# A graph-and-expert layer on one core: blank rows written in pieces, dispatched rows in two halves, result filled later

## The chip, the cores and the metric

The kernel runs on one core of a Trainium2 chip. The metric is the device time of one execution in microseconds; before and after are each run several times, and the median is compared. One further execution is profiled. All loops are unrolled in the program except some rarely taken ones.

## The reference

Input: 3125 nodes with 256 features, 53125 weighted edges sorted by target, weights of three sub-layers, all float32.

```python
xn = layernorm(x)
x = x + gnn(xn) + mix(xn)          # two rounds of sparse product, softmax, tanh; linear attention
h = layernorm(x)
probs = softmax(h @ gate_w + gate_b)      # 8 experts
idx, prb = argmax(probs), max(probs)
pos = (place of the token among those of its expert); kept = pos < 489
buf[e, pos] = h                           # a dispatch of rows to their expert's buffer
y = relu(buf @ w1 + b1) @ w2 + b2         # for each expert: 489 x 256 -> 1024 -> 256
x = x + nan_to_num(y[idx, pos] * prb * kept)
```

## The kernel before

Nodes stand in 25 tiles of 128 (the last has 53). `XX` holds, for each node, 514 words: the normalised row (256, `XN`), the row so far, which is the residual of the last step (256, `X1`), the gate's probability (`kp`), and the node's number (`ids`).

Stages, in the order of time. *Ranking* (until about 300 us of the span): the edges are sorted into blocks and the attention's products are formed. *Build*: the adjacency matrix is made as 157 units (four 128 x 128 blocks each, by one-hot products, TensorE line 1261), evacuated by ScalarE (line 619) to `RING`, applied at once to `XN` (line 1278, first of three sparse products), and stored to `adj_dram` by ScalarE's DMA queue as 32 chunks of five units (line 623). `RING` has two chunks for this, so the evacuation of chunk n + 2 waits for the store of chunk n. VectorE makes the one-hot tiles (`hots`, lines 886 to 895) ahead of TensorE, and between them copies finished node rows to `HB` (`hn_out`, line 906). *Strips*: the matrix is read back in chunks by SyncE's DMA queue (line 466) for two more sparse products of seven strips each (line 1411). In the second, each strip's nodes are finished, gated and dispatched. *Experts*: for each of eight, rows are loaded, flipped (line 1182), multiplied up (line 1493) and down (line 1504), and VectorE finishes four blocks of the result (`yblock`, from line 1162), which POOL scatters to `out` (line 552).

The dispatch: `xbuf_dram` has 8 x 512 rows of 514 words. Rows to which no node goes must read as zero with an impossible node number, so that their results are dropped. For this POOL writes a tile `blank`, 128 x 514 words, that lies in `hb[:, 5376:5890]`, over the attention's weights `wq_n` and `woT` (dead once the small products are done, line 992), and SyncE writes it over the whole of `xbuf_dram` in one DMA (line 394). Later `HB`'s tile 21 takes the same columns; so VectorE waits for that DMA (`s_xz`, line 994, step 40 of its loop). POOL waits for it before the first dispatch, then scatters each tile's 514-word rows (line 544). SyncE waits for all dispatches (`s_disp`), loads the normalised halves of two experts (`tokens`, line 439), then their residual halves (`kept_rows`, line 442).

Nodes over an expert's capacity of 489 get no expert result. So `out` is first filled with the residual rows (`before`, lines 446 and 448): tiles 0 to 19 when strips 0 to 4 are done, the rest after the first loads; POOL's scatters wait for the fills (`s_pre`).

The order of each engine's instructions is as written; an engine that waits holds all that is behind it. The same holds for SyncE, which issues most DMAs.

Of the kernel before, what the change touches and what calls it, by code (L numbers as in the profile page):

```python
# [9 lines left out]
I32 = mybir.dt.int32  # L10
ACT = mybir.ActivationFunctionType
AX_X = mybir.AxisListType.X
ds = bass.ds
# [10 lines left out]
ROW = 2 * 256 + 2  # L24
# [71 lines left out]
def graph_program(nc, a, out):  # L96
    ctx = ExitStack()
    with ctx:
        def sb(name, shape, dt=F32):
            return ctx.enter_context(nc.sbuf_tensor(name, shape, dt))  # L100

        def sem(name):
            return ctx.enter_context(nc.semaphore(name))

        def dram(name, shape, dt=F32):
            return nc.dram_tensor(name, shape, dt, kind="Internal").ap()
# [3 lines left out]

        xbuf_dram = dram("xbuf_dram", [NE * XS, ROW])

# [30 lines left out]
        blank = hb[:, 5376:5376 + ROW]  # L143
# [87 lines left out]
        kvc = sb("kvc", [P, 2])  # L231
        M = W[:, 3364:3876].rearrange("p (c n) -> p c n", c=2)
# [112 lines left out]
        s_disp = sem("s_disp")  # L345
        s_b2 = sem("s_b2")
# [37 lines left out]
        def _(sp):  # L384
# [9 lines left out]
            sp.dma_start(xbuf_dram.rearrange("(p c) d -> p c d", p=P), blank.unsqueeze(1).to_broadcast([P, NE * XS // P, ROW])).then_inc(s_xz, 16)  # L394
# [43 lines left out]
            def tokens(e, s):  # L438
                sp.dma_start(xbs[:, s, :, 0:D], xbuf_dram[ds(e * XS, XS), 0:D].rearrange("(c p) f -> p c f", p=P)).then_inc(s_wl[s], 16)

            def kept_rows(e, s):
                sp.dma_start(xbs[:, s, :, D:ROW], xbuf_dram[ds(e * XS, XS), D:ROW].rearrange("(c p) f -> p c f", p=P)).then_inc(s_res[s], 16)

            def before(t0, t1):
                last = min(t1, NT - 1)
                sp.dma_start(out[t0 * P:last * P, :].rearrange("(t p) d -> p t d", p=P), X1[:, t0:last, :]).then_inc(s_pre, 16)
                if t1 == NT:
                    sp.dma_start(out[last * P:N, :], X1[0:LAST, last, :]).then_inc(s_pre, 16)
# [22 lines left out]
            sp.wait_ge(s_var, NS - 1)  # L471
            before(0, 20)
# [6 lines left out]
            for s in range(2):  # L479
                kept_rows(s, s)  # L480
            sp.wait_ge(s_var, NS + 1)
            before(20, NT)
# [12 lines left out]
        def _(gp):  # L495
# [31 lines left out]
            gp.wait_ge(s_mv, 1)  # L527
            gp.memset(blank, 0.0).then_inc(s_blank, 1)
            gp.wait_ge(s_blank, 1)
            gp.memset(blank[:, 2 * D + 1:ROW].bitcast(I32), NOWHERE).then_inc(s_zero, 1)  # L530
# [8 lines left out]
            gp.wait_ge(s_xz, 16)  # L539
            for k in range(NS):  # L540
                gp.wait_ge(s_slot, k + 1)
                for j in STRIPS[k]:
                    n = P if j < NT - 1 else LAST
                    gp.indirect_dma_start(xbuf_dram[:, :], bass.IndirectOffsetOnAxis(ap=sidx[0:n, j:j + 1], axis=0),  # L544
                                          XX[0:n, j, :], None, bounds_check=NE * XS - 1, oob_is_err=False).then_inc(s_disp, 16)

            gp.wait_ge(s_pre, 16 * 3)
# [9 lines left out]
        def _(act):  # L557
# [136 lines left out]

            for k in range(NS):
                zout(0, k)
                ex(0, k)
                tanh(0, k)
# [43 lines left out]
        def _(dve):  # L742
# [3 lines left out]
            def link(ins):  # L746
                chain[0] += 1
                ins.then_inc(s_dve, 1)
                dve.wait_ge(s_dve, chain[0])
# [209 lines left out]
            for it in range(NU + 8):  # L959
# [33 lines left out]
                if it == NT + 15:  # L993
                    dve.wait_ge(s_xz, 16)
# [160 lines left out]
            def yblock(e, s):  # L1155
                for c in range(4):
                    n = min(P, CAPX - c * P)
                    y = ybs[0:n, s, c, :]
                    dve.wait_ge(s_y, 4 * e + c + 1)
                    if e >= 2 and c == 0:  # L1160
                        dve.wait_ge(s_out[s], 16 * 4 * (e // 2))
                    v.tensor_tensor(y, ps[0:n, 5 + c % 2, 0:D], b2_b[0:n, e * D:(e + 1) * D], ALU.add).then_inc(s_yv, 1)  # L1162
                    dve.wait_ge(s_yv, 4 * e + c + 1)
                    link(v.tensor_scalar(y, y, xbs[0:n, s, c, 2 * D:2 * D + 1], None, ALU.mult))
# [370 lines left out]
```

## Time and profile before

| | us |
|---|---|
| median of 3 runs | 1299.79 (1293.42 to 1300.66) |
| profiled execution | 1298.54 |
| its span | 1296.6 |
| TensorE busy | 1145.2 (88%) |
| VectorE busy | 737.5 (57%) |
| ScalarE busy | 326.1 (25%) |
| POOL busy | 109.0 (8%) |
| mean granted clock of TensorE | 0.947 of full speed |

In the profile PE is TensorE, DVE VectorE, ACT ScalarE, POOL GpSimd and SP SyncE. An engine's busy time is no measure of what it costs: only what lies on the chain of work that ended last sets the time. The granted clock is a share of 2.4 GHz. Times of rows are microseconds from the start of the span.

### The profile page before, as it was taken

The numbers are of one execution on the slowest core, as the hardware profiler recorded it, in microseconds if no ns is written. First come the engines' busy times: TensorE is split into PE (matmuls) and PEld (weight loads), VectorE is DVE, ScalarE is ACT, GpSimd is POOL, SyncE is SP. The second block draws the span as 40 slices with busy tenths as digits, with TensorE's granted clock in tenths as the row PEclk, the third lists the DMA queues.
The fourth block names the chain that finished last, engine by engine and source line by source line (L and its number), as shares of the span: only waits on it lengthen the run. The fifth ranks groups of instructions, "written<-read, shape, count | busy, mean of one in ns | idle before, by whom it ended". The sixth has DMA issues, their size and how long they took to land.

```text
span 1296.6 us, 14218 instructions
## 1 busy us (share of the span) xinstructions
PE 1145.2 (88%) x4999; PEld 725.3 (56%) x4999; DVE 737.5 (57%) x1711; ACT 326.1 (25%) x1028; POOL 109.0 (8%) x150
## 2 busy tenths in 40 slices
PE   1678988889379999999999799999999649999996
PEld 1345655666146666666668344454555526676664
DVE  5888988978067777777775011022345614455544
ACT  1445445431012121121212011111322412211220
POOL 1112112110000000000000000000112111111111
PEclk9799889899679999999999899999999759999998
DMA  6100101112941112211122898878897632333320
GB/s 161 11 4 41 42 1 41 41 41 74 252 137 82 81 82 85 119 82 82 82 93 110 300 375 295 301 278 303 224 343 258 210 124 88 119 113 108 117 99 9
DMA packets 61077, 175.38 MB, mean 135 GB/s; under 512 B 15990, under 2 KB 40285, under 8 KB 48974
## 3 DMA queue, kind: packets, MB, share of 16 engines
q1 hardware_dynamic: 46504, 120.70, 27.9%
q10 hardware_dynamic: 10598, 45.72, 9.0%
q0 software_dynamic: 3904, 8.03, 2.0%
q8 instruction: 42, 0.69, 0.2%
q14 instruction: 29, 0.24, 0.1%
HBM read 113.82 MB, written 63.01 MB: 136 GB/s over the span
## 4 chain that ended last, share of the span: by engine, by line
PE 80%; DVE 7%; ACT 5%; DMA 5%; issue 2%; SPq 0%; POOL 0%; POOLq 0%; DVEq 0%; ACTq 0%
PE ps L1411 21%; PE ps L1278 19%; PE ps L1261 11%; PE ps L1493 8%; PE ps L1504 8%; DMA xbuf_dram<-HB 3%; PE ps L1236 3%; ACT W L597 2%; PE ps L1182 2%; PE ps L1303 2%; ACT RING L609 1%; PE ps L1443 1%; PE ps L1222 1%; PE ps L1280 1%; DVE W L847 1%
## 5 line engine op out<-in xcount | busy, mean ns | idle before, releaser
L1278 PE MATMUL ps<-RING,XX 128*128 128x512 f32 x600 | 284.3, 596 | 0.2
L1411 PE MATMUL ps<-RING,RY 128*128 128x512 f32 (+1 forms) x700 | 277.0, 552 | 6.4 <-issue 6.4
L1261 PEld LDWEIGHTS ps<-RING 128*128 128x128 f32 x1250 | 163.8, 194 | 84.7 <-issue 81.9
L1261 PE MATMUL ps<-RING 128*128 128x128 f32 x1250 | 171.5, 278 | 39.8 <-DVE RING L895 30.8
L1411 PEld LDWEIGHTS ps<-RING,RY 128*128 128x128 f32 x700 | 124.9, 192 | 140.7 <-issue 140.7
L619 ACT COPY RING<-ps 128x512 f32<-128x512 f32 (+1 forms) x157 | 91.6, 584 | 368.6 <-PE ps L1261 352.5
L886 DVE TENSOR_TENSOR RING<-iota_n,RY 128x512 f32<-128x512 f32 (+1 forms) x157 | 107.8, 687 | 105.1 <-PE ps L1261 60.7
L1278 PEld LDWEIGHTS ps<-RING,XX 128*128 128x128 f32 x600 | 103.2, 192 | 73.1 <-issue 73.0
L892 DVE TENSOR_TENSOR RING<-iota_n,RY 128x512 f32<-128x512 f32 (+1 forms) x157 | 106.9, 681 | 0.0
L895 DVE TENSOR_TENSOR RING<-RING,RY 128x512 f32<-128x512 f32 x132 | 89.9, 681 | 0.0
L1162 DVE TENSOR_TENSOR W<-ps,RING 128x256 f32<-128x256 f32 (+1 forms) x32 | 13.4, 419 | 126.6 <-PE ps L1504 126.6
L544 POOL DMA_INDIRECT xbuf_dram<-XX,sidx x25 | 25.6, 1023 | 702.6 <-DVE sidx L1126 696.8
L733 ACT ACTIVATE RY<-ps,b1T 128x489 f32<-128x489 f32 x64 | 42.8, 670 | 162.3 <-PE ps L1493 162.3
L1049 DVE TENSOR_REDUCE nmx<-ps 128x4 f32<-128x512 f32 (+1 forms) x7 | 4.4, 635 | 115.5 <-PE ps L1182 115.5
L1504 PE MATMUL ps<-RING,RY 128*128 128x256 f32 (+1 forms) x256 | 56.3, 381 | 0.8 <-ACT RY L733 0.8
L1504 PE MATMUL ps<-XT,RY 128*128 128x256 f32 (+1 forms) x256 | 56.3, 381 | 0.0
L1493 PE MATMUL ps<-RING,XT 128*128 128x489 f32 x128 | 55.3, 591 | 0.7 <-ACT RING L726 0.7
L1236 PE MATMUL ps<-wkvT,XT 128*128 128x512 f32 x100 | 51.1, 636 | 3.7 <-ACT XT L588 3.7
L1493 PE MATMUL ps<-RING 128*128 128x489 f32 x128 | 53.1, 573 | 0.0
L1504 PEld LDWEIGHTS ps<-RING,RY 128*128 128x128 f32 (+1 forms) x256 | 47.1, 185 | 9.5 <-ACT RY L733 1.5
L847 DVE TENSOR_TENSOR W<-HB 128x468 bf16<-128x468 bf16 x125 | 51.9, 478 | 0.0
L1504 PEld LDWEIGHTS ps<-XT,RY 128*128 128x128 f32 (+1 forms) x256 | 47.1, 185 | 8.0
(232 smaller groups left out, 1300.0 us busy)
## 6 DMA issues: line engine op xcount, KB each, us to landing
RING<-adj_dram SPq DMA_DIRECT2D x62, 1280.0 KB, 6.0
adj_dram<-RING ACTq DMA_DIRECT2D x31, 1280.0 KB, 4.5
xbuf_dram<-HB SPq DMA_DIRECT2D x1, 8224.0 KB, 43.5
XT<-in_L_ffn_w SPq DMA_DIRECT2D x8, 1024.0 KB, 7.5
RING<-in_L_ffn_w SPq DMA_DIRECT2D x8, 1024.0 KB
RING<-xbuf_dram SPq DMA_DIRECT2D x8, 516.0 KB, 4.0
RING<-xbuf_dram SPq DMA_DIRECT2D x8, 512.0 KB, 5.3
XX<-in_x ACTq DMA_DIRECT2D x1, 3072.0 KB
```

Source lines behind the costliest of these rows:

```text
L619: nc.scalar.copy(RING[:, n % 2, u % 5 * 512:u % 5 * 512 + w], ps[:, bank_of(u), 0:w]).then_inc(s_bev, 1)
L733: nc.scalar.activation(hmT[:, f, 0:CAPX], ps[:, 2 + f % 3, 0:CAPX], ACT.Relu, bias=b1T[:, f, e:e + 1]).then_inc(s_hidv, 1)
L847: last = v.tensor_tensor(V[:, b, f * SW:(f + 1) * SW].rearrange("p (c s i) -> p c s i", s=NR, i=2), ohp[b].rearrange("p (c s i) -> p c s i ...
L886: v.tensor_tensor(h[:, 0, 0:n, :], every, grid(0), ALU.is_equal).then_inc(s_eq, 1)
L892: last = v.tensor_tensor(h[:, 1, 0:n, :], every, grid(1), ALU.is_equal)
L895: last = v.tensor_tensor(h[:, 0, 0:n, :], h[:, 0, 0:n, :], grid(2), ALU.mult)
L1236: last = nc.tensor.matmul(ps[:, PROD, :], XT[:, c, m * P:(m + 1) * P], wkvT[:, c, :], start=(c == 0), stop=(c == 1))
L1261: last = nc.tensor.matmul(o[:, i * P:(i + 1) * P], h[:, 0, i, :], h[:, 1, i, :], start=True, stop=(j != s))
L1278: last = nc.tensor.matmul(ps[:, ACC + dd, :], w, at, start=(j == 0), stop=True, skip_group_check=True)
L1411: last = nc.tensor.matmul(o, (Y if l == 0 else S0)[:, j, :], RING[:, slot_of[g % 5], i * w:(i + 1) * w], start=(j == 0), stop=(j == NT - 1 ...
L1493: last = nc.tensor.matmul(ps[:, 2 + f % 3, 0:CAPX], w1s[s][:, c, f * P:(f + 1) * P], xbT[:, s, c, 0:CAPX], start=(c == 0), stop=(c == 1))
L1504: last = nc.tensor.matmul(o, hmT[:, f, c * P:c * P + n], w2s[s][:, f, :], start=(f == 0), stop=(f == 7))
```

## The change

- `blank` moves to `W[:, 2048:2562]`, is written once `s_m` is reached (the small products are done), and VectorE's wait at step 40 is gone. ScalarE waits for all blank writes before the first sparse strip, whose results go to the same columns.
- `xbuf_dram` becomes two buffers: `xbuf_dram` with 256-word rows, and `rbuf_dram` with 258-word rows for residual, probability and number. SyncE writes the blanks in eight steps, an expert's 512 rows of both buffers at a time, after ScalarE's evacuations 44, 54, ... 114.
- POOL scatters 256-word rows for a strip's tiles, then the 258-word rows; those of strip 5 come behind the dispatches of strip 6.
- SyncE loads `tokens` for two experts after the first halves, waits for the second (`s_dres`), loads `kept_rows(0, 0)`, fills all of `out`, loads `kept_rows(1, 1)`.
- `yblock` multiplies `b2` by the probability before it waits for TensorE, and then forms product and sum in one operation on the PSUM tile.

```diff
--- before.py
+++ after.py
@@ -21,7 +21,8 @@
 NE = 8
 CAPX = 489
 XS = 512
-ROW = 2 * 256 + 2
+RES = 256 + 2
+ROW = 256 + RES
 NOWHERE = 1 << 20
 F = 1024
 NH = 8
@@ -108,7 +109,8 @@
 
         adj_dram = dram("adj_dram", [NC, P, 5 * 512])
 
-        xbuf_dram = dram("xbuf_dram", [NE * XS, ROW])
+        xbuf_dram = dram("xbuf_dram", [NE * XS, D])
+        rbuf_dram = dram("rbuf_dram", [NE * XS, RES])
 
 
         XX = sb("XX", [P, NT, ROW])
@@ -140,7 +142,6 @@
         ohp = [hb[:, 4806 + 234 * i:5040 + 234 * i].bitcast(BF16) for i in range(2)]
         wq_n = hb[:, 5376:5888].rearrange("p (r n) -> p r n", r=2)
         woT = hb[:, 5888:6400].rearrange("p (r n) -> p r n", r=2)
-        blank = hb[:, 5376:5376 + ROW]
 
         recs = RY[:, 0:5 * NG].rearrange("p (f n) -> p f n", f=5)
         S0 = RY[:, 0:NT * H].rearrange("p (t n) -> p t n", n=H)
@@ -229,6 +230,7 @@
         hrs = sb("hrs", [P, 2, KT * NH])
         hta = sb("hta", [P, KT * NH])
         kvc = sb("kvc", [P, 2])
+        blank = W[:, 2048:2048 + ROW]
         M = W[:, 3364:3876].rearrange("p (c n) -> p c n", c=2)
         nmx = sb("nmx", [P, 2, 4])
         rsum = sb("rsum", [P, 2, 4])
@@ -343,6 +345,7 @@
         s_cntr = sem("s_cntr")
         s_slot = sem("s_slot")
         s_disp = sem("s_disp")
+        s_dres = sem("s_dres")
         s_b2 = sem("s_b2")
         s_wl = [sem(f"s_wl{i}") for i in range(2)]
         s_res = [sem(f"s_res{i}") for i in range(2)]
@@ -391,7 +394,11 @@
                     for to, name in ((src_w, "src"), (dst_w, "dst"), (val_w, "edge_weight")):
                         sp.dma_start(to[:, ds(j * WC, WC)], a[name][ds(first, WIN)].rearrange("(p c) -> p c", c=WC)).then_inc(s_win[g], 16)
             sp.wait_ge(s_zero, 3)
-            sp.dma_start(xbuf_dram.rearrange("(p c) d -> p c d", p=P), blank.unsqueeze(1).to_broadcast([P, NE * XS // P, ROW])).then_inc(s_xz, 16)
+            for i in range(8):
+                sp.wait_ge(s_bev, 44 + 10 * i)
+                for to, cols in ((xbuf_dram, blank[:, 0:D]), (rbuf_dram, blank[:, D:ROW])):
+                    w = D if to is xbuf_dram else RES
+                    sp.dma_start(to[i * XS:(i + 1) * XS, :].rearrange("(p c) d -> p c d", p=P), cols.unsqueeze(1).to_broadcast([P, XS // P, w])).then_inc(s_xz, 16)
 
             sp.wait_ge(s_rounds, 1)
             with more_rounds(sp):
@@ -436,10 +443,10 @@
                 sp.dma_start(w2s[s], a["L0_ffn_w2"][ds(e, 1), :, :].rearrange("a (c p) f -> p (a c) f", p=P)).then_inc(s_wl[s], 16)
 
             def tokens(e, s):
-                sp.dma_start(xbs[:, s, :, 0:D], xbuf_dram[ds(e * XS, XS), 0:D].rearrange("(c p) f -> p c f", p=P)).then_inc(s_wl[s], 16)
+                sp.dma_start(xbs[:, s, :, 0:D], xbuf_dram[ds(e * XS, XS), :].rearrange("(c p) f -> p c f", p=P)).then_inc(s_wl[s], 16)
 
             def kept_rows(e, s):
-                sp.dma_start(xbs[:, s, :, D:ROW], xbuf_dram[ds(e * XS, XS), D:ROW].rearrange("(c p) f -> p c f", p=P)).then_inc(s_res[s], 16)
+                sp.dma_start(xbs[:, s, :, D:ROW], rbuf_dram[ds(e * XS, XS), :].rearrange("(c p) f -> p c f", p=P)).then_inc(s_res[s], 16)
 
             def before(t0, t1):
                 last = min(t1, NT - 1)
@@ -468,18 +475,16 @@
                         sp.wait_ge(s_mixp, NT)
                         weights(0, 0)
 
-            sp.wait_ge(s_var, NS - 1)
-            before(0, 20)
             sp.wait_ge(s_zc, 2 * NC)
             weights(1, 1)
             sp.dma_start(b2_b, a["L0_ffn_b2"].rearrange("e d -> (e d)").partition_broadcast(P)).then_inc(s_b2, 16)
             sp.wait_ge(s_disp, 16 * NT)
             tokens(0, 0)
             tokens(1, 1)
-            for s in range(2):
-                kept_rows(s, s)
-            sp.wait_ge(s_var, NS + 1)
-            before(20, NT)
+            sp.wait_ge(s_dres, 16 * NT)
+            kept_rows(0, 0)
+            before(0, NT)
+            kept_rows(1, 1)
             for e in range(NE - 2):
                 sp.wait_ge(s_xbt, 2 * (e + 1))
                 tokens(e + 2, e % 2)
@@ -524,10 +529,10 @@
                     gp.wait_ge(s_stats, NT)
                     gp.tensor_tensor(X1[:, it, :], X1[:, it, :], bo_b[:, :], ALU.add).then_inc(s_bo, 1)
 
-            gp.wait_ge(s_mv, 1)
+            gp.wait_ge(s_m, 1)
             gp.memset(blank, 0.0).then_inc(s_blank, 1)
             gp.wait_ge(s_blank, 1)
-            gp.memset(blank[:, 2 * D + 1:ROW].bitcast(I32), NOWHERE).then_inc(s_zero, 1)
+            gp.memset(blank[:, ROW - 1:ROW].bitcast(I32), NOWHERE).then_inc(s_zero, 1)
 
             gp.wait_ge(s_rounds, 1)
             with more_rounds(gp):
@@ -536,15 +541,19 @@
                     gp.wait_ge(s_ast[i], 16 * NC // 2)
                 gp.iota(e_int, pattern=[[1, NP]], base=0, channel_multiplier=0).then_inc(m_iota, 1)
 
-            gp.wait_ge(s_xz, 16)
+            gp.wait_ge(s_xz, 16 * 16)
             for k in range(NS):
                 gp.wait_ge(s_slot, k + 1)
                 for j in STRIPS[k]:
                     n = P if j < NT - 1 else LAST
                     gp.indirect_dma_start(xbuf_dram[:, :], bass.IndirectOffsetOnAxis(ap=sidx[0:n, j:j + 1], axis=0),
-                                          XX[0:n, j, :], None, bounds_check=NE * XS - 1, oob_is_err=False).then_inc(s_disp, 16)
-
-            gp.wait_ge(s_pre, 16 * 3)
+                                          XX[0:n, j, 0:D], None, bounds_check=NE * XS - 1, oob_is_err=False).then_inc(s_disp, 16)
+                for j in STRIPS[k] if k < NS - 2 else [] if k < NS - 1 else STRIPS[k - 1] + STRIPS[k]:
+                    n = P if j < NT - 1 else LAST
+                    gp.indirect_dma_start(rbuf_dram[:, :], bass.IndirectOffsetOnAxis(ap=sidx[0:n, j:j + 1], axis=0),
+                                          XX[0:n, j, D:ROW], None, bounds_check=NE * XS - 1, oob_is_err=False).then_inc(s_dres, 16)
+
+            gp.wait_ge(s_pre, 16 * 2)
             for e in range(NE):
                 for c in range(4):
                     n = min(P, CAPX - c * P)
@@ -692,6 +701,7 @@
                 act.wait_ge(s_tb, k + 1)
                 nc.scalar.activation(ta8[:, 0:w, :], tb8[:, 0:w, :], ACT.Exp).then_inc(s_exp8, 1)
 
+            act.wait_ge(s_xz, 16 * 16)
             for k in range(NS):
                 zout(0, k)
                 ex(0, k)
@@ -990,8 +1000,6 @@
                 if it == M_AT + 1:
                     dve.wait_ge(s_m, 1)
                     v.tensor_copy(M[:, :, :], ps[:, PROD, :].rearrange("p (c n) -> p c n", c=2)).then_inc(s_mv, 1)
-                if it == NT + 15:
-                    dve.wait_ge(s_xz, 16)
                 if it - 3 in HN_AT:
                     hn_out(HN_AT[it - 3])
                 if it - 3 in MIX_AT:
@@ -1156,12 +1164,13 @@
                 for c in range(4):
                     n = min(P, CAPX - c * P)
                     y = ybs[0:n, s, c, :]
-                    dve.wait_ge(s_y, 4 * e + c + 1)
+                    prob = xbs[0:n, s, c, 2 * D:2 * D + 1]
                     if e >= 2 and c == 0:
                         dve.wait_ge(s_out[s], 16 * 4 * (e // 2))
-                    v.tensor_tensor(y, ps[0:n, 5 + c % 2, 0:D], b2_b[0:n, e * D:(e + 1) * D], ALU.add).then_inc(s_yv, 1)
+                    link(v.tensor_scalar(y, b2_b[0:n, e * D:(e + 1) * D], prob, None, ALU.mult))
+                    dve.wait_ge(s_y, 4 * e + c + 1)
+                    v.scalar_tensor_tensor(out=y, in0=ps[0:n, 5 + c % 2, 0:D], scalar=prob, in1=y, op0=ALU.mult, op1=ALU.add).then_inc(s_yv, 1)
                     dve.wait_ge(s_yv, 4 * e + c + 1)
-                    link(v.tensor_scalar(y, y, xbs[0:n, s, c, 2 * D:2 * D + 1], None, ALU.mult))
                     v.tensor_scalar(nanm[0:n, 0, :], y, FMAX, None, ALU.is_gt)
                     v.tensor_scalar(nanm[0:n, 1, :], y, -FMAX, None, ALU.is_lt)
                     link(v.tensor_tensor(nanm[0:n, 2, :], y, y, ALU.not_equal))
```

## Rows read from the trace of the kernel before

**Rows 1.** The page, chain that ended last, by engine
```profile
PE 80%; DVE 7%; ACT 5%; DMA 5%; issue 2%; SPq 0%; POOL 0%; POOLq 0%; DVEq 0%; ACTq 0%
```

**Rows 2.** Sums by stretch: start:end, length, engine busy, PEclk, DMA share, GB/s
```profile
326.00:363.00 37.00, 8.08 (x38) 4.95 (x36) 0.18 (x1) 1.40 (x3) 0.00 (x0) 0.64 1.06 247
363.00:700.00 337.00, 334.85 (x1603) 222.70 (x1604) 252.87 (x449) 69.13 (x118) 0.00 (x0) 0.99 0.22 91
```

**Rows 3.** Chain in order of time, 319 to 384: start, us, what
```profile
319.28 43.51 DMA xbuf_dram<-HB
...
366.91 3.41 PE ps L1278 x4
370.32 1.00 PE ps L1261 x8
...
382.40 0.89 PE ps L1261 x8
383.29 1.72 PE ps L1278 x4
```

**Rows 4.** Timeline, 332 to 366: start, us, engine, line, shape, [idle before, releaser]
```profile
332.20 1.88 PE L1278 MATMUL ps<-RING,XX 128*128 128x512 f32 x4
...
362.82 0.69 DVE L886 TENSOR_TENSOR RING<-iota_n,RY 128x512 f32<-128x512 f32 x1 [38.36 <-DMA xbuf_dram<-HB]
...
364.86 2.05 PE L1261 MATMUL ps<-RING 128*128 128x128 f32 x8 [30.78 <-DVE RING L895]
```

**Rows 5.** Timeline of the hand-over, 1020 to 1057
```profile
1020.05 0.97 POOL L544 DMA_INDIRECT xbuf_dram<-XX,sidx  x1 [14.58 <-DVE sidx L1126]
...
1040.72 0.97 POOL L544 DMA_INDIRECT xbuf_dram<-XX,sidx  x1 [15.87 <-DVE sidx L1126]
...
1056.58 1.94 PE L1182 MATMUL ps<-ident,RING 128*128 128x128 f32 x8 [14.03 <-DMA RING<-xbuf_dram]
```

**Rows 6.** Chain in order of time, 1045 to 1057
```profile
1045.83 6.64 DMA xbuf_dram<-XX,sidx
1052.48 3.96 DMA RING<-xbuf_dram
```

**Rows 7.** Timeline of DVE and PE, first expert's block and the last expert's
```profile
1079.24 0.42 DVE L1162 TENSOR_TENSOR W<-ps,RING 128x256 f32<-128x256 f32 x1 [35.20 <-PE ps L1504]
...
1271.11 14.08 PE L1504 MATMUL ps<-RING,RY 128*128 128x256 f32 x64 [0.76 <-ACT RY L733]
1274.93 0.42 DVE L1162 TENSOR_TENSOR W<-ps,RING 128x256 f32<-128x256 f32 x1 [13.05 <-PE ps L1504]
1275.39 0.35 DVE L1164 TENSOR_SCALAR W<-W,RING 128x256 f32<-128x256 f32 x1
...
1286.03 0.42 DVE L1162 TENSOR_TENSOR W<-ps,RING 105x256 f32<-105x256 f32 x1
```

**Rows 8.** Line 623: its last nine issues (first, last start), and landing of all 32
```profile
L623 ACTq DMA_DIRECT2D adj_dram<-RING x9: 338/338/339, 607.7 to 713.8; - x9
...
DMA to landing us min/median/max: 4.4/4.5/13.5
```

**Rows 9.** The page, DMA issues: size and median time to landing
```profile
xbuf_dram<-HB SPq DMA_DIRECT2D x1, 8224.0 KB, 43.5
```

**Rows 10.** Sums by stretch, columns as in rows 2
```profile
1005.00:1010.00 5.00, 5.00 (x17) 2.41 (x16) 2.82 (x13) 0.20 (x1) 0.47 (x1) 1.00 0.79 271
...
1050.00:1052.00 2.00, 0.00 (x0) 0.00 (x0) 0.00 (x0) 0.00 (x0) 0.00 (x0) 0.50 0.06 24
...
1060.00:1065.00 5.00, 5.00 (x9) 2.10 (x8) 0.00 (x0) 0.85 (x2) 0.00 (x0) 0.67 0.76 269
```

**Rows 11.** Landing of line 439 (tokens); line 552 (scatter): duration, starts, landing
```profile
DMA to landing us min/median/max: 4.0/5.3/7.6
...
L552 POOL DMA_INDIRECT out<-W,RING x32: 966/972/1093, 1083.9 to 1290.7; - x32
...
DMA to landing us min/median/max: 2.1/2.5/7.7
```

## The prediction

> **What bounds the kernel now.** I read four views in this order. First the page's chain by engine [rows 1]: TensorE carries 80% of the span, so a change pays only where TensorE stands idle. Next the sums by stretch [rows 2]: TensorE is busy 8.08 of 37 us at 326 to 363, and 334.85 of 337 from there to 700. After 363 there is nothing to gain without less TensorE work; before it there is one hole of some 30 us.
>
> Third, what the hole consists of. The single zero fill `xbuf_dram<-HB` is issued at 319.28 and lands 43.51 us later [rows 3]; DVE, standing at its `s_xz` wait (line 994) because tile 21 of `HB` lies in the columns of `blank`, starts again at 362.82 after 38.36 us, so it had stopped at 324.46. TensorE had buffers for a few more units, ran dry after the matmuls at 332.20, and starts again at 364.86 [rows 4].
>
> Fourth, the hand-over from routing to the experts, where TensorE waits 14.03 us for the first token rows [rows 5, 6], and the end of the program, which is a row of DVE operations and a last scatter [rows 7].
>
> **Part 1: the blank moves, the DVE wait goes.** `blank` now lies in `W[:, 2048:2562]`, which is free from the end of the small products (`s_m`) until the first `zout`; the DVE wait is deleted; ScalarE waits for all 16 pieces before the first `zout`. What this gives is the distance between TensorE's groups. The group before the hole ends at 332.20 + 1.72 = 333.92. The next unit, one build and one apply, ends at 370.32, where the following build starts. A unit at the full clock is 0.89 + 1.72 = 2.61 us (the rows at 382.40 and 383.29), so 370.32 - 333.92 - 2.61 = 33.79 us go [rows 3, 4]. This already holds the price of the low clock: the stretch of the hole has a mean granted clock of 0.64 against 0.99 after it [rows 2], and the first apply group after 31 us of idleness takes 3.41 in place of 1.72, as at the 1.2 GHz level. The build after it still takes 1.00 in place of 0.89, another 0.11. Sum 33.9 us.
>
> What is late next there? DVE stopped at 324.46 while TensorE lived on its results until 333.92, so DVE was 9 us ahead, and it is the less busy of the two: 252.87 of 337 us in the stretch after the hole, which has the same units, node copies and mixes, against TensorE's 334.85 [rows 2]. It stays ahead. The new `s_m` wait on POOL costs nothing: POOL has no work between the blank and the dispatch, 600 us later.
>
> **Part 2: sixteen small writes beside the build.** On SP each pair (512 + 516 KB) waits for evacuation 44, 54, ... 114. What is queued behind them on SP is the first chunk load (g = 0) and the `rounds` branch, used only after 713; the stores of chunks 23 to 31 are issued from 607.7 on [rows 8], so evacuation 114, in chunk 22, lies before that. ScalarE's new wait stands behind evacuation 157 and is met by then: nothing. What the pieces can touch is the chunk stores of ScalarE. The fill's 8224 KB took 43.5 us [rows 9], so a pair is an eighth, 5.4 us; a store alone takes 4.5 [rows 8]. If the two simply add, the store lands after 9.9 us. It must have landed when the chunk after the next begins its evacuation, 6 units later, 6 x 2.61 = 15.7 us at least. The nearest row is harder than anything that the change makes: the longest store of all 32, that of 321.04 beside the whole fill and a chunk load, landed in 13.5 us [rows 8]. Cost 0; upper bound, a store that waits 13.5 and a full pair besides: 18.9 - 15.7 = 3.2 us for each of 8, 26 us. I see no way to a gain here.
>
> **Part 3: the dispatch in two halves.** Every tile is scattered as 1024-byte rows, the residual half follows; POOL issues 50 in place of 25. Strip 4's residual issues come behind its four dispatches (from 1020.05, 0.97 and a gap of 0.3 each): 8 x 1.28 = 10.2 us, done by 1030.3, before strip 5 needs POOL at 1040.72 [rows 5]. For strips 5 and 6 they come last, so the five dispatches keep their times. The last one, 53 rows, is issued at 1045.83 and lands 6.64 us later; only then SP issues `tokens(0,0)`, 3.96 us, and TensorE starts at 1056.58 [rows 5, 6]. At 1050 to 1052 the DMA share is 0.06 at 24 GB/s [rows 10]: 0.06 is one engine of sixteen, so these 53 rows drip through one engine. The shortest landing of an indirect issue is 2.1 us [rows 11]; 6.64 - 2.1 = 4.5 us is the drip, and with 1024 of 2056 bytes it is 2.3: gain 2.3 us. Bounds: 0 if the price is by the row, 4.5 if the drip vanishes. I take the half because 24 GB/s is what a busy engine moves elsewhere (269 GB/s at a share of 0.76 [rows 10] is 22 an engine), so bytes set the drip.
>
> The Trainium skill, "DMA: Bandwidth & Descriptors", section "Why a DMA increments its semaphore by 16 and not by 1", says that a DMA spreads over the largest number up to 16 that divides its outer dimension, hence one engine for 53 rows; the share of 0.06 agrees. By the same page's Specifications (27 GiB/s an engine) the last tile would take an estimated 3.8 us before and 1.9 after, 0.4 us less gain than my term.
>
> Against this: `tokens(0,0)` now runs beside the residual scatter (0.13 MB for each 1.28 us, some 100 GB/s) in place of beside other loads. I take 0.5 us, near the low end, since it ran beside more bytes before. Bounds 0 and 3.6 (the slowest of the tokens loads, 7.6 less 4.0 [rows 11]).
>
> **Part 4: the later residual loads and the result fill.** The residual issues end at about 1047.4 + 5 x 1.28 = 1053.8 and land by some 1058 with the same drip; `kept_rows(0,0)`, if it takes the slowest 7.6 of [rows 11], is there by 1066. DVE first needs it at 1079.24 [rows 7]: 13 us of cover. The whole fill of `out`, 3.2 MB, follows; at the 269 GB/s of [rows 10] it is 12 us, at the zero fill's 8224 KB in 43.5 us [rows 9] it is 17, so it ends at 1078 to 1083. POOL's first scatter waits for it and stood at 1083.9 [rows 11]. Were it late, POOL only catches up: DVE asks for its `s_out` two experts later. `kept_rows(1,1)` is wanted an expert after 1079. Cost 0. SP stands longer before `tokens(2,0)`, which TensorE flips after expert 1's up products only. Taking the early fill out of 1005 to 1015 gives nothing, since TensorE was busy all 5.00 us of 1005 to 1010 [rows 10].
>
> **Part 5: the yblock.** The product of `b2` and the probability now stands before the wait for TensorE. In the middle DVE is not the bound (it idles 13 us before an expert's first block). At the end it is: four blocks from 1274.93 on at a pitch of (1286.03 - 1274.93) / 3 = 3.70 us, slower than TensorE's 14.08 / 4 = 3.5. Only the first block's product comes off that path, 0.35 and its gap: 0.4 us [rows 7]. An operation with three operands on a PSUM tile isn't in the trace; I take the addition it replaces (0.42). Were each of four 0.4 us longer, 1.6 us would be lost instead of 0.4 gained.
>
> **The sum.** 33.9 + 2.3 - 0.5 + 0.4 = 36.1 us. The profiled execution took 1298.54 us (span 1296.6), so 1262.4. It lies 1.25 below the median of the three runs; from the median it is 1263.7. I give 1263.0.
>
> **Rivals.**
> (a) The stores are late beside the pieces (part 2). For it: no row shows a store beside a fill of 1 KB rows. Against: 13.5 us is below 15.7. It gives up to 1263 + 26 = 1289; chance 0.09.
> (b) The hand-over is off: the last tile lands in 2.1 us and tokens isn't slowed, 4.5 in place of 1.8, gives 1260; tokens 3.6 slower and no drip gained gives 1263 + 1.8 + 3.6 = 1268. Together 0.16.
> (c) Slower than before: twice the indirect issues hold up POOL. Between strip 4's first dispatch and strip 5's there are 1040.72 - 1020.05 = 20.7 us for 8 issues: from 2.58 us each on, the last dispatch is late. If each were held as long as the longest landing of an indirect one, 7.7 us [rows 11], the loss would be 61.6 - 20.7 = 41 us and the time 1304. Against: an issue takes 0.97 us [rows 5]. Chance 0.02. The Trainium skill, same page, section "SWDGE vs HWDGE vs iDMA", says that DVE in its two-port mode locks GpSimd out of the descriptor rings, which would be such a mechanism; the even 0.97 beside DVE's work doesn't show it.
> (d) The change doesn't do what it says: some engine on the build's path still waits for the fill. From the code only POOL's and ScalarE's later waits remain; 1298; chance 0.02.
>
> **How the numbers follow.** The forecast holds 0.71 (1257 to 1267), (a) 0.09, (b) 0.16, (c) 0.02, (d) 0.02. The range starts from the three runs of before: 1293.42 less 38.8 (33.9 + 4.5 + 0.4) is 1254.6; 1300.66 less 29.5 (33.9 - 3.6 - 0.8, the smallest without (a)) is 1271. So 1255 to 1271. 0.5% is 6.5 us, about what a measurement of this kernel can tell from no change. Faster by more: the forecast, (b) and nearly all of (a), 0.95. Within it: (d) and a little of (a), 0.03. Slower: (c), 0.02.
>
> **What would show it.** In the profile after: no idle time of DVE named `xbuf_dram` and TensorE busy throughout 320 to 370 (part 1); stores of line 623 below 10 us and ScalarE never waiting for one (part 2); the last dispatch landing in about 4.4 us, tokens in about 4.5 (part 3); DVE's idle time before the first `yblock` named PE, not a DMA (part 4); the time from the last expert's first PSUM read by DVE to the end 0.4 us shorter (part 5). I am wrong if TensorE shows a new gap at the chunk borders between 340 and 570, or if the chain of the hand-over runs through `rbuf_dram`.

## The result, and the profile after

| | before | changed |
|---|---|---|
| median, us (lowest to highest) | 1297.35 (1293.42 to 1300.66, 4 runs) | 1264.31 (1263.89 to 1265.38, 4 runs) |
| profiled execution | 1298.54 | 1263.89 |
| its span | 1296.6 | 1262.1 |
| mean granted clock of TensorE | 0.947 | 0.968 |

The ratio is 0.9748, with a 95% interval of 0.9714 to 0.9781. The changed kernel is faster by 2.5%, 33 us by the medians and 34.5 us by the two profiled spans. The line numbers of the changed kernel are 9 to 10 higher than before's: 1270 is the build's product (1261), 1287 the apply (1278), 1420 the strips (1411), 632 the chunk store (623), 1172 the first operation of the yblock that reads PSUM (1162).

The page's chain by engine. Against [rows 1], DMA has fallen from 5% to 2%, and nothing of a fill is in it:

```profile
PE 82%; DVE 7%; ACT 5%; issue 3%; DMA 2%; SPq 0%; POOL 0%; POOLq 0%; DVEq 0%; ACTq 0%
```

Sums by stretch, the columns of [rows 2]. The 37 us that held the hole are now full, at full clock, and so is the rest of the build:

```profile
326.00:363.00 37.00, 37.00 (x179) 24.64 (x178) 26.82 (x46) 7.55 (x13) 0.00 (x0) 1.00 0.27 100
326.00:655.00 329.00, 328.79 (x1582) 218.53 (x1581) 242.87 (x432) 67.44 (x115) 0.00 (x0) 1.00 0.31 118
```

The chain at the same place (start, us, what), where [rows 3] had 43.51 us of DMA. One build of 0.89 and one apply of 1.72 follow each other:

```profile
321.10 0.89 PE ps L1270 x8
321.99 1.72 PE ps L1287 x4
323.70 0.89 PE ps L1270 x8
324.60 1.72 PE ps L1287 x4
326.31 0.89 PE ps L1270 x8
327.21 1.72 PE ps L1287 x4
```

The landing of the 32 chunk stores (line 632, as line 623 in [rows 8]). The longest is 9.9 us; the prediction's worst simple case was 9.9 too:

```profile
L632 ACTq DMA_DIRECT2D adj_dram<-RING x32: 338/338/377, 108.1 to 679.1; - x32
...
DMA to landing us min/median/max: 4.4/4.6/9.9
```

The chain of the hand-over, as [rows 6]. The last dispatch lands in 4.37 in place of 6.64 us, the tokens load takes 4.60 in place of 3.96, and the first expert's up products 15.99:

```profile
1010.65 4.37 DMA xbuf_dram<-XX,sidx
1015.04 4.60 DMA RING<-xbuf_dram
1019.78 1.95 PE ps L1191 x8
...
1022.39 15.99 PE ps L1502 x32
```

The granted clock at the same distance from TensorE's first flip (1019.78) as the row 1060 to 1065 of [rows 10] has from its own (1056.58): 0.55 where it was 0.67. Both stretches hold the rise from the 1.2 GHz level; here it comes later.

```profile
1023.20:1028.20 5.00, 5.00 (x8) 2.18 (x7) 0.35 (x1) 0.67 (x1) 0.00 (x0) 0.55 0.87 265
```

The timeline of the first yblock, and of the last one with the end (as [rows 7]):

```profile
1026.85 0.35 DVE L1170 TENSOR_SCALAR W<-RING 128x256 f32<-128x256 f32 x1 [17.98 <-DMA RING<-rbuf_dram]
...
1042.98 0.48 DVE L1172 SCALAR_TENSOR_TENSOR W<-ps,RING,W 128x256 f32<-128x256 f32 x1 [15.78 <-PE ps L1513]
...
1238.70 0.48 DVE L1172 SCALAR_TENSOR_TENSOR W<-ps,RING,W 128x256 f32<-128x256 f32 x1 [13.09 <-PE ps L1513]
...
1254.15 0.97 POOL L561 DMA_INDIRECT out<-W,RING  x1 [2.80 <-DVE W L1180]
```

**Where the time went.** Cut both spans at one place, the issue of the last dispatch (1045.83 before, 1010.65 after). Ahead of it the changed kernel is 35.18 us shorter. Behind it, it is 0.68 us *longer*: 1262.1 - 1010.65 = 251.45 against 1296.6 - 1045.83 = 250.77. So the whole gain lies in the build, and the parts of the change that were to help the hand-over and the end gave nothing in sum. Their account, between the points of the profile: the dispatch lands 2.27 us sooner after its issue; the tokens load takes 0.64 longer; the first up products, at a clock that rises later, take 15.99 in place of 15.42, 0.57 longer; the yblock gives 0.31 (from VectorE's first read of PSUM for the last expert to the last scatter 15.45 us against 15.76); and from the last scatter's start to the end of the span it is 7.95 in place of 5.91 us, 2.04 longer. -2.27 + 0.64 + 0.57 - 0.31 + 2.04 = 0.67.

That last term is one row. POOL's closing instruction, which the profile names DRAIN, is 5957 ns long in the kernel before and 8000 ns in the changed one (name, count, duration min/median/max, start), the kernel before first:

```profile
L98 POOLq DRAIN  x1: 5957/5957/5957, 1290.4 to 1290.4; - x1
```

```profile
L99 POOLq DRAIN  x1: 8000/8000/8000, 1253.9 to 1253.9; - x1
```

### The profile page after: what moved, and what is told of

It reads as the page before. It is cut to its first block, busy times and chain, and to the rows that moved or that the text cites. A ratio compares the mean times of both kernels' runs of the same rounds, so it can differ in the third digit from the quotient of the medians.

```text
span 1262.1 us, 14314 instructions
## 1 busy us (share of the span) xinstructions
PE 1140.8 (90%) x4999; PEld 722.8 (57%) x4999; DVE 737.9 (58%) x1711; ACT 326.5 (26%) x1028; POOL 131.3 (10%) x175
## 4 chain that ended last, share of the span: by engine, by line
PE 82%; DVE 7%; ACT 5%; issue 3%; DMA 2%; SPq 0%; POOL 0%; POOLq 0%; DVEq 0%; ACTq 0%
PE ps L1420 21%; PE ps L1287 20%; PE ps L1270 11%; PE ps L1502 9%; PE ps L1513 8%; PE ps L1245 3%; ACT W L606 2%; PE ps L1191 2%; PE ps L1312 2%; ACT RING L618 1%; PE ps L1452 1%; PE ps L1289 1%; DVE W L857 1%; ACT RING L603 1%; DVE bst L953 1%
## 5 line engine op out<-in xcount | busy, mean ns | idle before, releaser
L1172 DVE SCALAR_TENSOR_TENSOR W<-ps,RING,W 128x256 f32<-128x256 f32 (+1 forms) x32 | 15.5, 484 | 108.3 <-PE ps L1513 107.4
L561 POOL DMA_INDIRECT out<-W,RING x32 | 31.4, 982 | 204.4 <-DVE W L1180 204.4
```

What stands on the lines that cost most here:

```text
L561: gp.indirect_dma_start(out[:, :], bass.IndirectOffsetOnAxis(ap=xbs[0:n, e % 2, c, 2 * D + 1:ROW].bitcast(I32), axis=0), ybs[0:n, e % 2, c ...
```

## The experiments

Three questions: is it the moved buffer or the eight pieces that frees the build; why the hand-over gained less than its landing; and what the 2.04 us at the end are. The span up to the last dispatch differs between executions of kernels with the same build by up to 3 us (1010.65 to 1013.62 in the eleven profiles without the hole, the changed kernel's among them). Most of it is there before the place of the hole: the chunk store that the changed kernel issues at 303.05 is issued at 305.93 in the run with the latest dispatch. So parts behind it are compared by the time from the last dispatch's issue to the end of the span, "behind the dispatch" below.

**e1: the blank moved, still one fill.** The kernel before with this edit (parts of lines and lines between are left out at `...`, here and below); the last line stands in ScalarE's program ahead of the first `zout`.

```diff
-        blank = hb[:, 5376:5376 + ROW]
+        blank = W[:, 2048:2048 + ROW]
-            gp.wait_ge(s_mv, 1)
+            gp.wait_ge(s_m, 1)
-                if it == NT + 15:
-                    dve.wait_ge(s_xz, 16)
...
+            act.wait_ge(s_xz, 16)
```

> The kernel before with one part of the change only: blank lies in W, VectorE's wait is gone, ScalarE waits before its first zout; the fill stays one DMA of 8224 KB, the dispatch whole. Theory (the stall was the buffer, not the size of the fill): TensorE busy throughout 320 to 370, span 33.8 us below before's 1296.6, so 1262.8; stores of line 623 and its like land within 13.5 us, below the 15.7 us that they have. Rival (the pieces are what frees the build): with one fill the two or three stores issued beside it land later than 15.7 us, ScalarE waits for one, and TensorE shows a gap of 3 to 20 us near 335 to 365; span 1266 to 1283.

Measured: median 1264.72 us (ratio 0.9722, 0.9696 to 0.9747), span 1262.9. The sums of the hole's stretch, and the landing of the stores:

```profile
326.00:363.00 37.00, 37.00 (x175) 24.25 (x174) 27.52 (x47) 7.54 (x13) 0.00 (x0) 1.00 1.04 271
```

```profile
L623 ACTq DMA_DIRECT2D adj_dram<-RING x32: 338/338/353, 107.8 to 680.4; - x32
...
DMA to landing us min/median/max: 4.4/4.5/15.7
```

The DMA share is 1.04, so the engines are as full with the fill as before, and TensorE doesn't notice: 37.00 of 37. The whole gain of the change is in these few lines; the theory holds. The expected bound of 13.5 us for a store was wrong, though. With the build going on the fill takes 52.7 us in place of 43.5, and four stores meet it in place of one; they land in 15.7, 11.7, 13.6 and 12.8 us. The longest is the first, issued at 321.32 as the one of 13.5 was at 321.04; why it took 2.2 us more isn't shown. It landed at 337.0, and ScalarE's next evacuation into its half of `RING` started at 337.97, waiting for TensorE and not for the store: 1.0 us was left. A fill of this size is near the edge.

**e2: the fill in eight pieces of whole rows.** On top of e1 (POOL's and ScalarE's waits count eight writes in place of one):

```diff
-            sp.dma_start(xbuf_dram..., blank...).then_inc(s_xz, 16)
+            for i in range(8):
+                sp.wait_ge(s_bev, 44 + 10 * i)
+                sp.dma_start(xbuf_dram[i * XS:(i + 1) * XS, :]..., blank...).then_inc(s_xz, 16)
```

> The same as e1 with the fill in eight pieces of whole 2056-byte rows at the evacuations 44, 54, ... 114; dispatch whole, as before. Theory: the span is within 0.5 us of e1's (pieces give nothing beside the moved buffer), and 1.6 to 2.3 us above the changed kernel's where the hand-over is counted (last dispatch issue to TensorE's first flip 10.75 us as before against 9.13). Rival: e2 is faster than e1 by the gap that e1 shows.

Measured: median 1263.55 (0.9714, 0.969 to 0.9737), span 1263.5. The longest store now lands in 9.7 us. The two medians lie 1.2 us apart with intervals that overlap: the pieces buy safety, and no time that these runs can show. From the last dispatch's issue to TensorE's first flip it takes 1023.61 - 1012.95 = 10.66 us, the changed kernel 9.13, so the changed kernel is 1.53 us ahead at the hand-over, a little less than the 1.6 to 2.3 expected. But it doesn't keep this: behind the dispatch, up to the end, this kernel takes 1263.5 - 1012.95 = 250.55 us and the changed one 251.45, 0.9 more.

**e3: the old fill, the rest of the change kept.** In the changed kernel, blank goes back, SyncE writes one fill for each of the two buffers as soon as `s_zero` is reached, VectorE waits for both, and ScalarE's wait is gone.

```diff
-        blank = W[:, 2048:2048 + ROW]
+        blank = hb[:, 5376:5376 + ROW]
...
-            for i in range(8):
-                sp.wait_ge(s_bev, 44 + 10 * i)
...
+                if it == NT + 15:
+                    dve.wait_ge(s_xz, 16 * 2)
```

> The changed kernel with blank, its two fills and VectorE's wait at the old place; dispatch in halves, late fill of out and new yblock kept. Theory: the hole is back, TensorE idle some 31 us; what stays of the gain is the hand-over (2.27 - 0.64 us) and the end (0.3 us), so 1.3 to 2.5 us below before. Rival (the gain is spread, the other parts carry some of it): 5 us or more below before. By 8192 shorter rows in the fill: if a row had a price of its own, the fill would take up to 87 us in place of 43.5 and this kernel would be up to 43 us slower than before.

Measured: median 1296.39 against 1299.1 for the kernel before (0.9971, 0.9958 to 0.9983), span 1293.4. The hole is back:

```profile
359.32 0.69 DVE L893 TENSOR_TENSOR RING<-iota_n,RY 128x512 f32<-128x512 f32 x1 [35.70 <-DMA rbuf_dram<-HB]
...
361.37 2.05 PE L1269 MATMUL ps<-RING 128*128 128x128 f32 x8 [28.11 <-DVE RING L902]
```

It is 28.11 us in place of the 30.78 of [rows 4]. The two fills are issued at 318.45 and 319.19 and the second lands at 359.30, so the same bytes in 8192 rows of 1024 and 1032 bytes took 40.85 us, 2.7 less than the 43.51 in 4096 rows of 2056. So there is no sign of a price by the row, which could have doubled the time. Why it was shorter isn't shown: the traffic beside it wasn't the same, since SyncE issued the chunk load at 333.82 and not at 321.22. The median is 2.7 us below before's, the span 3.2, a little more than the 1.3 to 2.5 expected, and not for the reason given: what this kernel gains on before is the shorter hole; behind the dispatch it takes 1293.4 - 1041.69 = 251.71, 0.9 more than before. So here too the other parts are worth nothing in sum.

**e4: the old yblock.** The changed kernel with the addition and the product both behind the wait for TensorE.

```diff
-                    link(v.tensor_scalar(y, b2_b..., prob, None, ALU.mult))
                     dve.wait_ge(s_y, 4 * e + c + 1)
-                    v.scalar_tensor_tensor(out=y, in0=ps..., scalar=prob, in1=y, op0=ALU.mult, op1=ALU.add).then_inc(s_yv, 1)
+                    v.tensor_tensor(y, ps..., b2_b..., ALU.add).then_inc(s_yv, 1)
                     dve.wait_ge(s_yv, 4 * e + c + 1)
+                    link(v.tensor_scalar(y, y, prob, None, ALU.mult))
```

> The changed kernel with the yblock of before. Theory: from the last expert's first PSUM read by VectorE to the last scatter 15.76 us in place of 15.45, so 0.3 us slower than the changed kernel at the end and nothing else. Rival (the last 6.98 us after the last scatter, 2.0 longer than before, hang on the new yblock): the end is 4.9 again and the span 1.7 us shorter than the changed kernel's.

Measured: median 1266.44 (0.9744, 0.9713 to 0.9774), span 1263.2. From VectorE's first PSUM read to the last scatter:

```profile
1239.41 0.42 DVE L1170 TENSOR_TENSOR W<-ps,RING 128x256 f32<-128x256 f32 x1 [13.05 <-PE ps L1512]
...
1255.17 0.97 POOL L561 DMA_INDIRECT out<-W,RING  x1 [2.80 <-DVE W L1179]
```

15.76 us, to the hundredth that of before, against 15.45. The new yblock is worth 0.3 us by these rows; the medians (1266.44 against 1264.31) can't show so small a part. POOL's drain is still 7998 ns, so the rival falls.

**e10: twenty more indirect issues.** On top of e2, in POOL's dispatch loop; POOL also waits for the 20 to have landed before its first scatter to `out`:

```diff
+                for j in STRIPS[k] if k < NS - 2 else []:
+                    gp.indirect_dma_start(spare[:, :], ...sidx[:, j:j + 1]..., XX[:, j, :], ...).then_inc(s_spare, 16)
```

> The kernel of e2 with 20 indirect issues added to strips 0 to 4, each writing a tile once more to a spare buffer that nothing reads. Theory (each indirect issue adds 82 ns to POOL's closing drain, from 5957 ns with 57 issues to 8000 ns with 82): drain 5957 + 20 x 81.7 = 7591 ns, the span 1.6 us longer than e2's 1263.5. Rival (the longer drain comes from the second DRAM buffer or the added semaphore that splitting brings): this kernel has a second buffer and a semaphore too, and the drain is 8000 ns; second rival (it comes from the rows' layout): 5957 ns.

Measured: span 1265.8, median 1266.9 (two runs). The drain:

```profile
L98 POOLq DRAIN  x1: 7590/7590/7590, 1258.0 to 1258.0; - x1
```

7590 ns, where 57 issues (25 dispatches and 32 scatters to `out`) give 5957 and 82 give 8000: three points on one line of 82 ns an issue. Behind the dispatch it takes 1265.8 - 1013.62 = 252.18 us, 1.63 more than e2, the same as the drain. The last extra issue starts at 996.7, 261 us before the drain, and all had landed before the first scatter to `out`, so it isn't their transfers that the drain waits for. Nor is it the number of rows: the changed kernel with 75 rows more in each half (e5 below) has 7994 ns, and the kernel with whole rows and 75 rows more (e9 below) 5952. It is the number of issues. This explains the 2.04 us.

**e5: the last tile as 128 rows.** In the changed kernel, both scatters:

```diff
-                    n = P if j < NT - 1 else LAST
+                    n = P
```

> The changed kernel, with tile 24 dispatched as 128 rows in both halves in place of its 53 (the 75 rows beyond the nodes carry numbers from 3125 on and are dropped by the last scatter). Theory (the last dispatch is slow because its 53 rows drip through one DMA engine): it lands in 2.1 to 2.6 us in place of 4.37, TensorE starts 1.8 to 2.3 us earlier after it, span 1260. Rival (it is slow for being the last of a backlog of five issues): with 75 rows more it lands no earlier, 4.4 us or a little later.

Measured: median 1263.66 (0.9723, 0.9705 to 0.9741), span 1261.6. The chain of its hand-over:

```profile
1012.87 2.21 DMA xbuf_dram<-XX,sidx
1015.10 4.67 DMA RING<-xbuf_dram
```

128 rows land in 2.21 us, 53 rows took 4.37: the slow part was not the backlog, which is unchanged, and with the 0.06 of [rows 10] it is the one engine. 0.63 us of the difference is in POOL's issue itself, which takes 1.60 us for 53 rows, in the kernel before too, and 0.97 for 128. Behind the dispatch 1261.6 - 1012.87 = 248.73 in place of 251.45, 2.7 less. Of this 2.16 is the landing and 0.65 the first up products (15.34 in place of 15.99), which were no part of the theory. By the medians, 1263.66 and 1264.31 from different series, the gain isn't shown. The span is 1.6 us above the 1260 expected, since 2.2 us more lie ahead of the dispatch than in the changed kernel.

**e9: whole rows, the last tile as 128 rows.** e2 with the edit of e5 in its one scatter.

> The kernel of e2 (blank moved, pieces, whole rows of 514 words) with tile 24 dispatched as 128 rows. Theory (one engine's drip; POOL's closing drain grows with the number of indirect issues): the last dispatch lands in 2.5 to 3.2 us in place of 6.59, POOL's closing drain stays 5.96 us since no issue is added, span 1263.5 - 3.7 = 1259.8, which is below the changed kernel's 1262.1 by 2.3. Rival (halving the rows is what speeds the hand-over): the landing stays above 5.5 us, span 1262.5 to 1263.5.

Measured: median 1260.91 (0.9707, 0.9689 to 0.9726), span 1257.9.

```profile
1011.01 2.53 DMA xbuf_dram<-XX,sidx
1013.56 3.97 DMA RING<-xbuf_dram
```

Whole rows of 2056 bytes land in 2.53 us once they are spread over the engines; the tokens load takes 3.97 again, and the drain 5952 ns. Behind the dispatch 246.89 us, 4.6 less than the changed kernel. The expectation of a gain of 3.7 on the kernel with 53 rows (250.55) came out: 3.66. The span is 1.9 us below the 1259.8 expected, all of it ahead of the dispatch (1011.01 against 1012.95).

**e11: e9 with the new yblock.**

> The kernel of e9 (blank moved, pieces, whole rows, tile 24 as 128 rows) with the new yblock. Theory: the new yblock takes 0.3 us off the end and nothing else changes: span 1257.9 - 0.3 = 1257.6, last scatter to end 6.0 us, and 4.5 us (0.35%) below the changed kernel's 1262.1. Rival (the product ahead of the wait delays the release of PSUM, so TensorE waits in the down products): the distance between the experts' down products grows above 27.96 us.

Measured in five runs: median 1260.2 (0.9693, 0.9673 to 0.9713), span 1258.2. The last expert's stretch takes 1252.24 - 1236.80 = 15.44 us against 15.70 in the kernel without it, and the experts keep their distance of 27.96. The span is 0.6 us above the expected 1257.6. By the profiles it is the shortest behind the dispatch, 246.79, though only 0.1 below e9. Its median is 4.1 us below the changed kernel's, but the two intervals of the ratio (0.9673 to 0.9713 and 0.9714 to 0.9781) were taken beside different runs of before. So what it gains on the changed kernel, 4.7 us behind the dispatch, rests on the rows, not on a comparison of the two side by side.

**e7: residual halves after the tokens.** In POOL's program of the changed kernel:

```diff
+                if k == NS - 1:
+                    gp.wait_ge(s_wl[0], 48)
                 for j in STRIPS[k] if k < NS - 2 else [] if k < NS - 1 else ...:
```

> The changed kernel, but POOL scatters the residual halves of strips 5 and 6 only when tokens(0, 0) has landed. Theory (the residual scatter beside it is what slows the tokens load): tokens lands in 3.96 us as before in place of 4.60; kept_rows comes 4 to 5 us later, VectorE's first product waits until about 1031, still before TensorE's first result at 1043; span 0.6 us shorter than the changed kernel's. Rival (tokens is slower for another reason, the rows' new layout in DRAM): it stays at 4.6.

Measured: span 1264.4, median 1266.07 (two runs).

```profile
1017.72 3.79 DMA RING<-xbuf_dram
...
1024.25 16.45 PE ps L1504 x32
```

The load takes 3.79 us; in the six kernels that scatter residual halves beside it, it takes 4.25 to 4.74. So the scatter beside it was what slowed it. But the first up products take 16.45 in place of 15.99 us, and behind the dispatch it is 251.13, only 0.3 less than the changed kernel, where 0.6 was expected; the span is 2.3 us longer, all of it ahead of the dispatch. VectorE's first product, which waits for `kept_rows`, starts at 1036.40 (expected: 1031), and TensorE's first result is there at 1045.3: still hidden.

**e8: the early fill of `out`.** The changed kernel with `before(0, 20)` at its old place, `before(20, NT)` at the new one.

> The changed kernel with the fill of out for tiles 0 to 19 at its old place, beside the last strip. Theory (part 4 of the prediction, the fill is hidden at both places): the span is the changed kernel's, 1262.1, within 0.5; SP's issue of the second part of the fill no longer takes 6.35 us. Rival (the early fill delays the last chunk loads or the last dispatches): TensorE's last strip ends 1 us or more later, or the first dispatch of strip 5 lands later.

Measured: span 1264.4, median 1265.69 (two runs); behind the dispatch 1264.4 - 1013.07 = 251.33 against 251.45. The 2.3 us of span are all ahead of the dispatch, and 2.2 of them are there at 300 us, long before the fill of `out` (the apply group that the changed kernel starts at 302.40 starts at 304.64). Neither place costs anything that these runs can show.

**e6: four times the bytes in the pieces.** In the changed kernel, in each of the eight steps, after the two blank writes:

```diff
+                for r in range(3):
+                    sp.dma_start(spare[r, i]..., blank...).then_inc(s_spare, 16)
```

> The changed kernel with four times the bytes in each of the eight steps (three more writes of whole blank rows to a spare buffer), 4.2 MB and by the fill's rate some 21 us each. If stores and pieces simply add (rival (a) of the prediction), the store behind each step lands after 4.5 + 21 = 25.5 us, 9.8 us beyond its 15.7, and the kernel is 8 x 9.8 = 78 us slower than the changed one. If the DMA engines serve the two queues in turn, a store lands in 9 to 16 us, as the 13.5 and 15.7 us of the stores beside the whole fill, and TensorE loses nothing or up to 1 us a step: span 1262 to 1270.

Measured: span 1263.2, median 1265.72 (two runs). Sums of the build's middle and the landing of its 17 stores:

```profile
340.00:590.00 250.00, 249.79 (x1198) 166.09 (x1197) 183.43 (x327) 51.02 (x88) 0.00 (x0) 1.00 0.71 227
```

```profile
L636 ACTq DMA_DIRECT2D adj_dram<-RING x17: 337/338/348, 350.3 to 587.9; - x17
...
DMA to landing us min/median/max: 4.5/7.9/12.5
```

Not one matmul waits: 249.79 of 250 us, the very number of the changed kernel's stretch. The three spare writes of a step land in 14.9 us (median), so a step is some 15 to 20 us of transfer (an estimate from when they are issued and land), and a store issued into it lands in 7.9 (median) to 12.5 us. Store and fill don't add up, so the store on ScalarE's queue is served beside the writes on SyncE's. The Trainium skill, "DMA: Bandwidth & Descriptors", section "Queues, rings and completion order", says that each DMA engine takes the queues with work in turn, packet by packet; the 12.5 us in place of an added 25.5 agree with it. Rival (a) of the prediction is out, since even these steps stop nothing.

## Why the prediction was right, and where it was not

The forecast was 1263.0 us in a range of 1255 to 1271; measured, 1264.31. The main mechanism, the buffer that holds up the build, was right and was the whole gain. The total is closer than the parts: an error of 2.9 us behind the dispatch is partly made up by 1.0 us ahead of the hole that the change has no hand in, and that is luck. By its steps:

- *What bounds the kernel* and *part 1* (33.9 us). Right in mechanism and size. The span up to the last dispatch shrank by 35.18 us, of which 1.0 us lies ahead of the hole: the third apply group after 295 starts at 302.40 where it was 303.41. In the hole and behind it 34.2 remain against 33.9. Over all eleven profiles without the hole the span to the last dispatch is 32.2 to 35.2 us shorter. The run with the moved buffer alone shows that this term needs no other part.
- *Part 2* (0). Right: no store came later than 9.9 us, and TensorE is full. The upper bound of 3.2 us a step wasn't reached even with four times the bytes. What the prediction didn't see is the reverse, that the eight pieces weren't needed either: one fill gives the same time, though its longest store landed only 1.0 us before its buffer was wanted.
- *Part 3, the landing* (gain 2.3). Measured 2.27, and the one-engine drip is borne out by the run with 128 rows (2.21 us for more than twice the rows). The step "with 1024 of 2056 bytes it is 2.3" holds: counted against the landing of 128 rows, the 53 cost 4.06 us with whole rows (6.59 less 2.53) and 2.16 with halves (4.37 less 2.21). What I drew from it didn't go far enough: the drip can be taken away without splitting anything, and whole rows then land in 2.53. The estimate from the Trainium skill, "DMA: Bandwidth & Descriptors", section "Specifications", a gain of 1.9 us, was the worse of the two against the 2.27 measured.
- *Part 3, the tokens load* (loss 0.5). Measured 0.64, and by e7 and e9 it comes from the residual scatter beside it: 3.79 us without it, 3.97 with whole rows.
- *Part 4* (0). Right, though its sign in the profile was named wrongly. I expected VectorE's idle time ahead of the first yblock to be put down to PE; it is put down to `RING<-rbuf_dram`, since the product now stands first. The residual rows were there at 1026.85, TensorE's result at 1042.98: 16 us of cover, 13 were forecast. The late fill blocked SyncE's queue for 6.35 us and more, which nobody waited for.
- *Part 5* (gain 0.4). Measured 0.31, since the operation with three operands takes 0.48 us where I took 0.42.
- *Missing from the sum*: 2.04 us at the end. I counted POOL's 25 further issues only where they are issued, between two strips, and not in the program's closing drain, where each costs 82 ns more. The row for it (5957 ns) was in the trace of before and I didn't ask what it grows with. This is the largest error of the sum. Missing too: 0.57 us at the first up products, from a clock that rises later. They take between 15.29 and 16.45 us in the thirteen profiles. Their length goes with how long TensorE had stood idle before its first flip, but not one way: 15.3 to 15.4 us after 13.9 to 14.0 us of idleness, 16.0 to 16.2 after 12.1 to 12.6, 16.45 after 11.6, and 15.3 to 15.7 after 9.9 to 10.3. So from 14 down to 11.6 us, about half of what an earlier start gains is lost again in these products, and the prediction counted it whole. No run was made to test this.
- *The range*. Its upper end takes 0.8 us off for the yblock, where part 5 had worked out 1.6 lost; with 1.6 it would be 1272. It decided nothing here.

Sum of the forecast 36.1, measured 34.5 in spans: 0.3 and 1.0 more than forecast in and ahead of the build, 2.9 less behind the dispatch (0.68 lost where 2.2 were to be gained: 2.04 the drain, 0.57 the clock, 0.3 tokens, landing and yblock together). By the medians it is 33.0, because before's median moved to 1297.35 with its fourth run; in the series of the experiments it was 1299.1, 1299.9 and 1298.98, and the profiled run from which the forecast was worked out, 1298.54, is close to these. Rival (b) didn't come: the landing and the tokens load were within 0.2 us of their terms. Rival (c) was right to look at more indirect issues, but not at POOL's issue time, which stayed at 0.97 us for 128 rows; rival (d) is out.

## What to carry to other kernels

A wait on a long transfer can be a wait for the columns it reads, as here: look first whether the tile can lie elsewhere, before the transfer is cut up or split. Count a DMA three times, where it is issued, where it lands, and, for indirect ones, in the closing drain of the engine that issued them; and give an indirect scatter on the path a row count that spreads over all DMA engines (128 rows here, not 53), even if some rows are thrown away. Cut two profiles at one shared event and compare the parts: here the total agreed with the forecast while one half of the change had given nothing.

## What the runs showed of the hardware that I had not expected

- POOL's closing drain takes 5952 to 5957 ns with 57 indirect issues, 7590 with 77 and 7994 to 8000 with 82, wherever in the program they stand: 82 ns each, on the path. The number of rows doesn't move it.
- An indirect scatter of 53 rows of 2056 bytes lands in 6.5 to 6.6 us, one of 128 such rows in 2.5 to 2.8. POOL's issue of it takes 1.60 us for 53 rows and 0.97 for 128.
- 8.4 MB of blanks landed in 40.9 us in 8192 rows of 1 KB and in 43.5 us in 4096 rows of 2 KB, each beside one chunk store, and in 52.7 us in 4096 rows beside four.
- A 1280 KB store issued beside 4.2 MB of other writes on another queue lands in at most 12.5 us (4.5 alone), and beside one fill of 8.4 MB in up to 15.7.
